# Four graph layers on one core: exponentials turned unweighed, sums multiplied by reciprocals when read from PSUM, diagonal overwritten in DRAM, chunks turned to banks of their own

## The reference

```python
L0: y = (adj @ x + x) @ weight + bias;  y / max(norm(y), EPS)
L1: five times: m = adj @ h;  gates z, r and candidate hv from m and h;  h = (1 - z) * h + z * hv
L2: A = adj + eye;  d = A.sum(-1) ** -0.5;  (d[:, None] * A * d[None, :]) @ x @ W.T + b
L3: A = where(adj > 0, e[0][cumsum(adj > 0) - 1], NEG);  A = softmax(A, axis=1)
    (A * eye) @ (x @ W[0]) + (A * (1 - eye)) @ (x @ W[1]) + bias
```

## Time and profile before

| | |
|---|---|
| median of 3 runs | 767.0 us (765.65 to 767.03) |
| the profiled execution | 765.98 us, span 763.6 us |
| TensorE busy | 748.1 us (98%) |
| VectorE busy | 629.8 us (82%) |
| ScalarE busy | 512.1 us (67%) |
| GpSimd busy | 163.3 us (21%) |
| mean granted clock of TensorE | 0.999 |
| DMA | 16.86 MB, 6.2% of the engines' time in the kernel's queue |

### The profile page before, as it was taken

The page is one execution under the profiler, slowest core; times in us unless marked ns, Lnnn a source line. Parts: engine busy times, 40 slices in busy tenths (PEclk is TensorE's granted clock), DMA queues, the critical chain, the costliest instruction groups (busy, mean ns, idle before and its releaser), DMA issues.

```text
span 763.6 us, 11935 instructions
## 1 busy us (share of the span) xinstructions
PE 748.1 (98%) x3764; PEld 626.5 (82%) x3764; DVE 629.8 (82%) x1458; ACT 512.1 (67%) x1069; POOL 163.3 (21%) x309
## 2 busy tenths in 40 slices
PE   7999999999999999999999999999999999899996
PEld 6888788888888888888888888888887888788886
DVE  5899998888888998877777777887999999686654
ACT  4799877666666676666666666666587858874444
POOL 1778520000000000000000000000123257764343
PEclk9999999999999999999999999999999999999999
DMA  6500000000030001000000000000000000000112
GB/s 215 216 1 2 1 1 1 1 1 1 0 118 14 1 2 56 1 0 1 1 0 0 0 0 0 0 1 2 1 0 2 1 1 1 15 1 29 56 56 84
DMA packets 10566, 16.86 MB, mean 22 GB/s; under 512 B 3472, under 2 KB 5008, under 8 KB 9872
## 3 DMA queue, kind: packets, MB, share of 16 engines
q1 hardware_dynamic: 10512, 16.20, 6.2%
HBM read 8.85 MB, written 5.25 MB: 18 GB/s over the span
## 4 chain that ended last, share of the span: by engine, by line
PE 80%; DVE 8%; ACT 7%; issue 2%; POOL 2%; DMA 1%; SPq 0%; POOLq 0%; ACTq 0%; DVEq 0%
PE agg_ps L1053 12%; PE agg_ps L1055 12%; PE agg_ps L1054 12%; PE gate_ps L974 7%; PE gate_ps L976 6%; PE gate_ps L975 6%; PE cand_ps L974 4%; PE cand_ps L976 4%; PE cand_ps L975 4%; PE turn_ps L1092 4%; PE gate_ps L981 3%; PE cand_ps L981 2%; ACT res L441 2%; ACT feat L518 1%; PE turn_ps L1096 1%
## 5 line engine op out<-in xcount | busy, mean ns | idle before, releaser
L1053 PE MATMUL agg_ps<-adj_hi,nat_hi 128*128 128x512 f32 x384 | 152.2, 396 | 0.0
L1055 PE MATMUL agg_ps<-adj_hi,nat_lo 128*128 128x512 f32 x384 | 150.1, 391 | 0.0
L1054 PE MATMUL agg_ps<-adj_lo,nat_hi 128*128 128x512 f32 x384 | 149.6, 390 | 0.0
L649 POOL TENSOR_SCALAR shift<-mean_var 128x4 f32<-128x4 f32 x62 | 24.7, 399 | 424.1 <-DVE mean_var L874 421.8
L503 ACT ACTIVATE reset_hi<-gate_r 128x512 fp32r<-128x512 f32 x80 | 50.6, 633 | 82.7 <-DVE gate_r L841 82.7
L824 DVE TENSOR_TENSOR agg_lo<-agg_ps,agg_hi 128x512 fp32r<-128x512 f32 x80 | 55.2, 690 | 57.7 <-ACT agg_hi L470 57.7
L1055 PEld LDWEIGHTS agg_ps<-adj_hi,nat_lo 128*128 128x128 f32 x384 | 72.0, 188 | 16.3
L1054 PEld LDWEIGHTS agg_ps<-adj_lo,nat_hi 128*128 128x128 f32 x384 | 72.2, 188 | 15.5
L487 ACT ACTIVATE gate_r<-gate_ps,bias 128x512 f32<-128x512 f32 x80 | 55.2, 690 | 44.2 <-PE gate_ps L976 44.1
L1053 PEld LDWEIGHTS agg_ps<-adj_hi,nat_hi 128*128 128x128 f32 x384 | 72.1, 188 | 15.4 <-DVE adj_lo L898 0.3
L470 ACT ACTIVATE agg_hi<-agg_ps 128x512 fp32r<-128x512 f32 x80 | 48.7, 608 | 44.0 <-PE agg_ps L1055 43.7
(11 more groups left out here) (199 smaller groups left out, 1788.7 us busy)
## 6 DMA issues: line engine op xcount, KB each, us to landing
res<-in_x SPq DMA_DIRECT2D x16, 256.0 KB, 5.7
out<-res SPq DMA_DIRECT2D x16, 256.0 KB, 2.0
rows<-in_adj SPq DMA_DIRECT2D x4, 256.0 KB, 4.5
adj_hi<-eye_hi SPq DMA_DIRECT2D x1, 1024.0 KB, 9.9
adj_lo<-eye_lo SPq DMA_DIRECT2D x1, 1024.0 KB, 11.7
later<-in_adj SPq DMA_DIRECT2D x1, 1024.0 KB, 6.5
mix_rows<-mix SPq DMA_DIRECT2D x1, 1024.0 KB, 8.0
later<-mix_rows SPq DMA_DIRECT2D x1, 1024.0 KB, 4.8
```

What stands on the lines that cost most here:

```text
L1053: pe.matmul(ps, nat_hi[:, b, k, :], m_hi[:, k, :], start=(k == 0), stop=False)
L1054: pe.matmul(ps, nat_hi[:, b, k, :], m_lo[:, k, :], start=False, stop=False)
L1055: last = pe.matmul(ps, nat_lo[:, b, k, :], m_hi[:, k, :], start=False, stop=(k == T - 1))
```

## The change

Six things.

1. **Chunks to banks of their own.** Each adjacency chunk is turned into one `prep_ps` bank, copied and subtracted when it is turned. Unit 0 takes its twelve products in the order four hi hi, four lo hi (features' remainder), four hi lo (matrix's remainder). The zero matmuls run twice.
2. **Owner** is turned in slot 4 in place of 3.
3. **Additions.** In slot 17 unit 14 is added ahead of 13 (`ADDED` gives the order to those who wait).
4. **ScalarE's first half of a norm** stands behind the reset gate and `feat_hi` in its slot.
5. **Diagonal in DRAM.** The diagonal of the logits is read at about 286 us, then overwritten in DRAM with -3e38, so the exponentials of the reloaded block have zeros there. GpSimd subtracts the maxima of the diagonal in slot 80, ScalarE takes its exponential in slot 99, and VectorE adds it to the row sums. The selects and the warm activation are gone.
6. **Exponentials turned unweighed.** The blocks are turned without the scaling (`EXP_AT` 101, `MIX_AT` 105), read at the head of the next slot. The reciprocals and the diagonal's shares go to DRAM together and come back as `share_rows`. In L3 VectorE reads the sums from PSUM and multiplies them by the reciprocals (`agg_all`), where ScalarE copied them.

```diff
-OWNER_AT = 3
+OWNER_AT = 4
-EXP_AT = AFTER + 6
+DIAG_AT = LAST
+DIAG_EXP_AT = AFTER + 3
+EXP_AT = AFTER + 5
 INV_AT = EXP_AT + T
-MIX_AT = INV_AT + 2
+MIX_AT = EXP_AT + T
...
+            cells = mix_dram.rearrange("n m -> (n m)")[0:N * N:N + 1].rearrange("(p t) -> p t", t=T)
+            sp.wait_ge(const_made, consts)
             sp.wait_ge(mix_stored, 16)
+            sp.dma_start(diag[:, :], cells, allow_slow_non_contiguous=True).then_inc(diag_in, 16)
+            sp.wait_ge(diag_in, 16)
+            sp.dma_start(cells, lowest[:, :], allow_slow_non_contiguous=True).then_inc(diag_cut, 16)
+            sp.wait_ge(diag_cut, 16)
             sp.wait_ge(l2_lo_made, T)
             sp.dma_start(later[:, :, :], mix_dram.rearrange("(p t) m -> p t m", t=T)).then_inc(mix_loaded, 16)
...
-            sp.wait_ge(exp_inv_made, 1)
-            sp.dma_start(mix_dram[0].rearrange("(t p) -> p t", p=P), diag[:, :],
-                         allow_slow_non_contiguous=True).then_inc(diag_stored, 16)
-            sp.wait_ge(diag_stored, 16)
+            sp.wait_ge(shares_made, 2)
+            sp.dma_start(mix_dram[0:2].rearrange("a (t p) -> p a t", p=P), shares[:, :, :],
+                         allow_slow_non_contiguous=True).then_inc(shares_stored, 16)
+            sp.wait_ge(shares_stored, 16)
...
-            act.wait_ge(x_in[0], 16)
-            act.activation(nat_hi[:, 0, :, :], res[:, 0, :, :], ACT.Copy).then_inc(x_hi_made, 1)
-            for k in range(T):
-                act.wait_ge(eye_turned, k + 1)
-                act.activation(eye_hi[:, k, :], prep_ps[k][:, :], ACT.Copy).then_inc(eye_hi_made, 1)
+            for t in range(T):
+                if t == T - 1:
+                    act.wait_ge(x_in[0], 16)
+                    act.activation(nat_hi[:, 0, :, :], res[:, 0, :, :], ACT.Copy).then_inc(x_hi_made, 1)
+                act.wait_ge(eye_turned, t + 1)
+                act.activation(eye_hi[:, :, t * P:(t + 1) * P], prep_ps[t][:, :].rearrange("p (k i) -> p k i", k=T),
+                               ACT.Copy).then_inc(eye_hi_made, 1)
...
             def slot(s, ahead):
+                k = s - 1 - MIX_AT
+                if 0 <= k < T:
+                    n = TURN_NO["mix", k]
+                    act.wait_ge(turned, n + 1)
+                    act.wait_ge(agg_done, AFTER)
+                    act.activation(adj_hi[:, k, :], turn_ps[n % 2][:, :], ACT.Copy).then_inc(mix_hi_made, 1)
...
-                if s < UNITS:
+                if s < UNITS - B:
                     act.wait_ge(agg_done, ahead(s + 1))
...
+                if s == DIAG_EXP_AT:
+                    act.wait_ge(diag_less_max, 1)
+                    act.activation(diag[:, :], diag[:, :], ACT.Exp).then_inc(diag_exp_made, 1)
...
-                if s == INV_AT:
-                    act.wait_ge(exp_inv_made, 1)
-                    for k in range(T // 2):
-                        act.wait_ge(diag_apart, k + 1)
-                        act.activation(later[:, k, :], later[:, k, :], ACT.Copy,
-                                       scale=exp_inv[:, k:k + 1]).then_inc(mix_made_act, 1)
...
-                for n in norms_at(s, "add"):
-                    i, b = NORMED.index(n), n % B
+                for n in sorted(norms_at(s, "add"), key=lambda n: stage(n) == L0 and n < B - 2):
+                    b = n % B
...
                 if s == INV_AT:
+                    dve.wait_ge(exp_made, T)
+                    dve.wait_ge(diag_exp_made, 1)
+                    link(dve.tensor_tensor(exp_sum[:, :], exp_sum[:, :], diag[:, :], ALU.add))
+                    dve.reciprocal(shares[:, SHARE_REST, :], exp_sum[:, :]).then_inc(shares_made, 1)
+                    dve.wait_ge(shares_made, 1)
+                    dve.tensor_tensor(shares[:, SHARE_DIAG, :], diag[:, :], shares[:, SHARE_REST, :],
+                                      ALU.mult).then_inc(shares_made, 1)
+                if UNITS - B <= s < UNITS:
+
+                    if s == UNITS - B:
+                        dve.wait_ge(agg_hi_made, s)
+                        dve.wait_ge(share_rows_in, 16)
+                    dve.wait_ge(agg_done, s + 1)
+                    dve.wait_ge(gate_done, s - 1)
+                    dve.tensor_tensor(agg_all[:, s % 2, :], agg_ps[s % 2][:, :], share_rows[:, SHARE_REST, :],
+                                      ALU.mult).then_inc(agg_hi_made, 1)
...
-            for ps in layer_ps:
+            for ps in layer_ps + layer_ps:
...
                     elif kind == "mix":
-                        pe.wait_ge(mix_made, T // 2)
-                        pe.wait_ge(mix_made_act, T // 2)
+                        pe.wait_ge(exp_made, T)
                         last = turn_rows(to, later, i)
```

More of the change, by code:

```diff
@@ L207, in graph_layers @@
             pass
-        with nc.sbuf_tensor("diag_row", [P, N], F32) as diag_row:
+        with nc.sbuf_tensor("share_rows", [P, 2, N], F32) as share_rows:
             pass
@@ L244, in graph_layers @@
         shift = sb("shift", [P, RING, T])
[L245 to L247 removed]
+        e_last = sb("e_last", [P, 1])
+        row_sum, row_d, row_max, exp_sum, diag, lowest = (sb(n, [P, T]) for n in
+                                                          ("row_sum", "row_d", "row_max", "exp_sum", "diag", "lowest"))
+        SHARE_DIAG, SHARE_REST = range(2)
+        shares = sb("shares", [P, 2, T])
         before, upto = (gate_r[:, 1, i:i + 1] for i in range(2))
@@ L478, in slot @@
                                    bias=bias[:, B_H:B_H + 1]).then_inc(cand_made, 1)
-                for n in norms_at(s, "norm"):
-                    if by_dve(n) == 0 and n < UNITS - 1:
-                        norm(n, 0, T // 2)
                 u = s - 1
@@ L497, in slot @@
                     act.activation(feat_hi[:, :], feat[:, s % B, :], ACT.Copy).then_inc(feat_hi_made, 1)
+                for n in norms_at(s, "norm"):
+                    if by_dve(n) == 0 and n < UNITS - 1:
+                        norm(n, 0, T // 2)
                 u = s - 1
@@ L657, in slot @@
                     pool.tensor_tensor(row_d[:, :], row_sum[:, :], half[:, :], ALU.pow).then_inc(row_d_made, 1)
-                for k in range(s - EXP_AT, s - EXP_AT + 1):
-                    if 0 <= k < T:
-                        pool.wait_ge(exp_made, k + 1)
-                        pool.affine_select(later[:, k, :], later[:, k, :], pattern=[[1, N]], compare_op=ALU.not_equal,
-                                           fill=0.0, base=-k, channel_multiplier=-T).then_inc(diag_apart, 1)
+                if s == DIAG_AT:
+                    pool.wait_ge(max_made, T)
+                    pool.wait_ge(diag_in, 16)
+                    pool.tensor_tensor(diag[:, :], diag[:, :], row_max[:, :], ALU.add).then_inc(diag_less_max, 1)
             run(pool, slot)
@@ L1047, in slot @@
                     b, ps = s % B, agg_ps[s % 2][:, :]
-                    for k in range(T):
-                        if s == 0:
-                            pe.wait_ge(eye_lo_made, k + 1)
-                        if s == AFTER + B:
-                            pe.wait_ge(turn_read, reads(TURN_NO["mix", k]))
-                        pe.matmul(ps, nat_hi[:, b, k, :], m_hi[:, k, :], start=(k == 0), stop=False)
-                        pe.matmul(ps, nat_hi[:, b, k, :], m_lo[:, k, :], start=False, stop=False)
-                        last = pe.matmul(ps, nat_lo[:, b, k, :], m_hi[:, k, :], start=False, stop=(k == T - 1))
+                    if s == 0:
+                        pe.wait_ge(eye_lo_made, 1)
+                        pe.wait_ge(eye_hi_made, T)
+                        pe.wait_ge(x_hi_made, 1)
+                        for k in range(T):
+                            pe.matmul(ps, nat_hi[:, b, k, :], m_hi[:, k, :], start=(k == 0), stop=False)
+                        pe.wait_ge(x_lo_made, 1)
+                        for k in range(T):
+                            pe.matmul(ps, nat_lo[:, b, k, :], m_hi[:, k, :], start=False, stop=False)
+                        pe.wait_ge(eye_lo_made, T)
+                        for k in range(T):
+                            last = pe.matmul(ps, nat_hi[:, b, k, :], m_lo[:, k, :], start=False, stop=(k == T - 1))
+                    else:
+                        for k in range(T):
+                            if s == AFTER + B:
+                                pe.wait_ge(turn_read, reads(TURN_NO["mix", k]))
+                            pe.matmul(ps, nat_hi[:, b, k, :], m_hi[:, k, :], start=(k == 0), stop=False)
+                            pe.matmul(ps, nat_hi[:, b, k, :], m_lo[:, k, :], start=False, stop=False)
+                            last = pe.matmul(ps, nat_lo[:, b, k, :], m_hi[:, k, :], start=False, stop=(k == T - 1))
                     last.then_inc(agg_done, 1)
```

96 lines of the change are left out of this document (36 added, 60 removed).

## The result

The changed kernel takes 760.81 us (median of 4 runs, 760.62 to 761.36), the kernel before beside it 766.33 (765.45 to 767.03): ratio 0.9921, 95% interval 0.9907 to 0.9935. Of its terms, those ahead of the second layer hold to a tenth or two; the term of the mixing stage was 3.6 us and measures 2.2. Against the profiled execution, with which the sum was made (765.98), the forecast was 760.2, and the profiled execution after took 761.36.

A forecast was written before the change was run, and what follows sets the result against it. TensorE, busy 748.1 of 763.6 us, bounds the kernel, so gains come from its idle time: 0.86 + 0.81 + 0 + 0.5 + 3.6 = 5.8 us. Forecast 760.2 against the profiled execution, 761.2 against the median, range 758.7 to 764.8.

The forecast's parts named there:

- The start: Kernel start: with chunks 0 to 2 copied as they come, unit 0 starts at 9.85 us, gaining 0.86.
- The owner turn: Layer one's start: moving the turn from slot 3 to slot 4 removes a TensorE loss of 0.81 us.
- The additions' order: Hand-over from layer one: TensorE's wait at 84.27 us shrinks but is waited at 95; gain 0, ends 0 and 0.82.
- The half norm: Late recurrent steps, 590.71 us: ScalarE's norm moves behind the reset gate; gain 0.5 us, ends 0 and 0.8.
- The mixing stage: Second layer's products, with the table load: waits of 1.07, 0.76, 2.41, 0.31 go, 0.95 comes; gain 3.6 us.
- GpSimd is done some 1.75 us sooner: Before ScalarE's slot 104: select removed (0.7) and VectorE's statistics up to 1.07 earlier, so the fourth exponential runs from 648.1.
- The shares: DRAM transfers in the second layer: 15 us, landing at 667; a landing up to 671.9 costs nothing.
- The last stage: Final stage: 16 copies move from ScalarE to VectorE as multiplications on read; cost nothing, uncovered 11 us in all.
- a new wait in place of the old: Second rival, mixing stage: ScalarE's slots 104 to 106 stay, turns wait 2.7 and 1.2 us; 764.1 us, chance 0.15.
- 2.7 us: First mix turn: upper end of its wait, if ScalarE's slot does not move; the wait was priced at 0.95.
- 6.3 us: Unit 110's seed: TensorE's wait if the shares land at 679.9; a slower rival at 769.3 us, chance 0.04.
- The first rival: First mix turn and layer-one additions: the wait hardly comes and the order pays; gain 7.5, 759.7 us, chance 0.17.

The follow-up runs named there:

- seed_one_input: Changed kernel with VectorE's seeds of units 96 to 126 reading one SBUF operand instead of two, leaving out later layers' biases; 760.29 us, one execution.
- shares_late: Changed kernel with the load of the shares waiting for one more TensorE turn, the back turn of slot 110; 765.10 us, one execution.

## Why the forecast was right, and where not

*The start:* 0.80 us for 0.86. *The owner turn:* 0.87 for 0.81. *The additions' order:* 0.05 for 0. *The half norm:* 0.40 for 0.5. These four are 2.1, which is the gain at unit 96 (616.22 less 614.13). Unit 0's start alone moves by 0.6 us between profiles and there is one of the kernel before, so the 0.80 is known no better than that; without it the other three are 1.32, and the distance from 0 to 96 shrinks by 1.29. ScalarE's and VectorE's chains from 43 to 95 us passed everything on: 1.67 us ahead at unit 7, 1.70 at 95.43. The products with zeros, costed at nothing to 0.2, cost nothing.

*The mixing stage* is the term that was mis-sized: 2.2 us (64.70 less 62.48) for 3.6. Its gains are all there: unit 101's copy (1.07), unit 107's (0.76), the first back turn (2.41). So is the weight load's at 680.10 (0.31). The losses are larger. The first mix turn takes 1.84 us for 0.95, and unit 103's copy, for which the forecast had nothing, 0.35; that gives 2.36, and 0.14 is left open. The step that failed is "GpSimd is done some 1.75 us sooner". ScalarE's slot 104 began 2.62 us sooner (645.09 for 647.71), and 2.09 of these had been won before the stage, so 0.53 is left of the 1.75. My sum took GpSimd's norms at the lengths of the kernel before; in the changed one they collide with VectorE's two-operand seeds: the two ahead of slot 104 take 2.63 and 2.37 us, 1.96 and 2.27 in the kernel before, 2.06 and 2.04 with seeds of one operand. In that kernel (seed_one_input, one execution) slot 104 begins 1.83 us sooner, counted from unit 96's layer product as the 0.53 above, the turn's loss is 0.97, and the stage gains 3.50 us (64.70 less 61.20). So the collision is nearly the whole difference. The forecast also priced a select at 0.7 us, and selects put back cost 0.29; how much of that is hidden by the collision no run shows.

*The shares:* cost nothing, as forecast, with the wait where it was named once they are made late (shares_late). Their price was 15 us and measures 14.5 from the first issue to the landing (10.7 from issue to issue, and 3.8). Inside it both parts were off: the store took 2.6 us more than that of 512 words, the load did not grow with its bytes. The forecast's reading that the words move within a microsecond was right, but what follows them grew, in finer windows of the same view: from 652.25 to the next issue at 661.26 it is 9.0 us, and 6.9 before (655.75 to 662.65). The Trainium skill ("DMA: Bandwidth & Descriptors", its table of where the fixed cost goes) has most of a small transfer's time in the receipt of the write; it gives the table for transfers issued from GpSimd, and these come from SyncE. The traces agree that the time lies behind the words; that it therefore stays at 8.2, as the forecast concluded, they do not show. Nor does the number of words decide: the diagonal's 512 words, one to a row, landed in 2.9. What does decide is open: no run changes only the place of the words. *The last stage* costs nothing: 4.99 us from unit to unit there, before and after.

*What has no run of its own:* the chunks' own banks, the moved table load and the earlier splits. Their waits are gone from the trace, by about the amounts forecast; that is all that is shown.

*The sum* against the profiled execution was too good by 1.2 us (760.2 for 761.36), and nearly all of it is the mixing stage. Against the median the forecast is within 0.4, because the medians stand 5.5 us apart and the two profiled executions 4.6; that the slower executions of the kernel before made up for most of what the mixing stage lacked is luck. The runs of the kernel before scatter over 765.45 to 768.95, those of the changed one over 760.62 to 761.53. In the profile of before the wait of 2.25 left the clock alone:

```profile
666.00:668.00 2.00, 0.13 (x2) 0.00 (x0) 0.37 (x1) 2.00 (x7) 0.71 (x2) 1.00 0.25 82
669.00:672.00 3.00, 3.00 (x17) 2.50 (x16) 2.96 (x12) 2.70 (x8) 1.61 (x3) 1.00 0.00 0
```

Waits of 1.99 and 2.31 lowered it in two other kernels, for 1.5 to 1.7 us. That it falls in some executions of the kernel before would explain their scatter; no profile of such an execution was taken, so it stays open. The mean granted clock on record fits: 0.997 to 1.000 in its executions of 765.77 to 766.11 us, 0.995 in the five of 768.47 to 768.95, and 0.995 or 0.996 in the three kernels above whose clock fell once. If so, part of what the change wins in the median is that it removes the wait of 2.25.

*The rivals:* a new wait in place of the old was half right, since the first turn is late, but the second and third turns are not. The forecast was also wrong in what a long wait costs: its "2.7 us" and "6.3 us" lack the 1.5 us of the clock that such waits brought here. The first rival's 759.7 is a slip: 767.0 less 7.5 is 759.5.

## What to carry to other kernels

When work is taken out of a chain of engines, find what each engine waited for: the exponentials cost nothing where ScalarE stood waiting for GpSimd, and 1.84 us at the end of slots in which it was already late, one to two slots further on. An operation of GpSimd on four columns is not of fixed length, so a norm that goes through VectorE, GpSimd and ScalarE should have slack; how much is not shown (no run here varies it). And allow for the clock when you price a wait of TensorE: 1.99 and 2.31 us cost another 1.71 and 1.57 here, 2.25 in the kernel before cost nothing.

## What had not been expected of the hardware

- Behind idle times of 1.99, 2.31 and 4.76 us TensorE's granted clock fell to 0.5 (1.2 GHz) and came back some 3 us later; that cost 1.71, 1.57 and 1.47 us. Behind 1.61 to 1.70 (seven profiles) and one of 2.25 it did not fall, so the length of the idle time alone does not decide.
- In the first 5 us the clock's row says 1.00, but products with zeros of 512 columns start 0.43 us apart (2.13, 2.98 and 3.83 for pairs), the spacing of the lower level. So the spacing, and not the clock's row, tells the level there.
- A GpSimd operation of 0.20 to 0.24 us took 0.41 to 0.82, and a power of 1.04 took 1.32 to 1.61, when VectorE ran an operation with two operands in SBUF as it began or just behind (and 2.22 at 608.41, while four such operations ran). With one operand the seed took the same 0.69 us and the longest power near it 1.12.
- 1024 single words side by side in DRAM took 10.7 us from issue to the next issue where 512 took 8.2; 512 words one to a row landed in 2.7 to 3.4 (13 profiles). A broadcast of 512 KB landed in 3.8 (3.3 in another run) where 256 KB took 4.8.
